# Retention's output projection in three rounded products, with norm and gate written in place

## The chip, the cores and the metric
The kernel runs on one core of a Trainium2 chip. A core has a matrix engine (TensorE, PE in the profile; its weight loads are PEld), a vector engine (VectorE, DVE), a scalar engine (ScalarE, ACT), GpSimd (POOL) and a queue that starts transfers (SyncE, SP). Each runs its own instructions in order and waits for the others through semaphores. The metric is the device time of one execution in microseconds; the median of three runs of the kernel before is 1364.03 us (1363.96 to 1365.25).

## The reference, cut to what matters
The program is a block of four layers on x of shape (4, 1024, 256): retention, a mixture of experts, a recurrence, and a mixture of experts again. Only retention is touched by the change:

```python
x = x + retention(layernorm(x))          # x: (4, 1024, 256)
# retention(x):
qkv = x @ w_qkv.T ; q, k, v = split(qkv) # 16 heads of 16; q, k rotated by position
scores = q k^T * 16**-0.5 * decay mask   # causal, decaying by head
y = scores @ v
yn = (y - mean) / sqrt(var + 1e-5)       # over (16 channels, 1024 tokens) of a head and batch
yn = yn * gn_weight + gn_bias
out = silu(x @ w_gated.T) * yn
return out @ w_proj.T
```

The statistics of the group norm run over all 1024 tokens of a batch element, so norm, gate and output projection of one batch element can't begin before its last token is done.

## The kernel before
Everything is float32 in memory. Tokens are handled in 32 tiles of 128, eight tiles (t = 0 to 7) to each of the four batch elements (b = 0 to 3); i counts tiles over all. Each engine has a hand-written order, a loop over i, in the function `retention`.

TensorE's loop, for tile i: transpose the normed x (L422), outputs of tile i-2 (state products L518, score by value products L524, into the PSUM bank ps_yp), project tile i to q, k (L444, L448) and v (L454), scores of tile i-1 (L484), the gate of tile i (L462), transposes of the rotated q and k (L473). The projections to q, k, v are already done "by parts": x and the weights are each a rounded part (high, type float32r, which TensorE takes in one pass) and a rest (low, the difference, also rounded), and three products are added, high by high, high by low, low by high. High parts of x are made by ScalarE (L345) together with the plain copy (L347); VectorE makes the low part (`x_low`, L623) from both; TensorE needs it at L448.

VectorE's loop: add the state product, norm the next tile's x (L616), rotate q and k (L634, L636; GpSimd adds the two halves, L291, before TensorE may transpose), add a finished pair of the projection to x (L725), mask the scores (L643), statistics, spread q (`spread_q`, L651), `x_low` of the next tile (L623).

While batch b runs, batch b-1 is finished: the group norm's statistics at t = 1 to 3; at t = 4 ScalarE writes the normed values (`normed`, L388, four instructions of 128x512, two before the gate's output and two after the q/k copy L373) into a buffer ynorm, and VectorE multiplies them by the gate (`gated`, L719): the first half after the mask, the second half after x_low of the next tile. At t = 5, 6, 7 and once more at t = 7 TensorE projects a pair of tiles (`projection`, L541), with plain float32 products of ynorm and w_proj; each such product is recorded as two matmuls. y itself lies in yt, double-buffered by batch. The last batch is finished behind the loop, with the PSUM banks of the scores.

Beside this the experts' weights are split for the next layer in 12 pieces: SP loads a piece, ScalarE rounds it at the end of its tile when i is odd, 5 to 27 (`split_high`, L380), GpSimd subtracts at the end of its tile when i is even, 6 to 28 (`split_low`, L305), and SP stores both parts.

Of the kernel before, what the change touches and what calls it, by code (L numbers as in the profile page):

```python
# [11 lines left out]
P = 128  # L12
# [14 lines left out]
def one_pass(ap):  # L27
    return ap.bitcast(mybir.dt.float32r)
# [23 lines left out]
def retention(nc, d, x, x_loaded, x_stats, w_split, home):  # L52
    with ExitStack() as ctx:
# [14 lines left out]

        qk_high, qk_low = (sb(f"qk_{n}", [P, KT, 2 * C]) for n in ("high", "low"))
        v_high, v_low = (sb(f"v_{n}", [P, KT, C]) for n in ("high", "low"))  # L70
        w_gate = sb("w_gate", [P, KT, C])
        w_proj = sb("w_proj", [P, KT, C])
        rope_cos = sb("rope_cos", [P, TPB, 2 * C])
# [28 lines left out]
        state_add = sb("state_add", [P, KT, PAIR])  # L102
        yt = sb("yt", [P, 2, KT, T])
        silu_g = sb("silu_g", [P, 2, KT, T])
        ynorm = sb("ynorm", [P, KT, T])
        gn_stats = sb("gn_stats", [P, KT, 2, 6])
        gn_sum = sb("gn_sum", [P, KT])
        gn_dev = sb("gn_dev", [P, KT, 4])
# [62 lines left out]
        gn_root = sem("gn_root")  # L171
        ynorm_ready = sem("ynorm_ready")
        gated_ready = sem("gated_ready")
        out_in_psum = sem("out_in_psum")
        x_added = sem("x_added")
        x_stats_ready = sem("x_stats_ready")
# [50 lines left out]
        with nc.Block() as block:  # L227
# [43 lines left out]
            @block.gpsimd  # L271
            def _(pool):
                pool.memset(expo[:], -0.5).then_inc(zeroed, 1)
                pool.memset(v_heads[:], 0.0).then_inc(zeroed, 1)
                pool.wait_ge(zeroed, 2)

                def ln_root_first():
                    pool.wait_ge(first_moments, MOMENT_STEPS)
                    pool.tensor_tensor(rstd[:, 0:1], vare[:, 0:1], expo[:, 0:1], ALU.pow).then_inc(first_rstd, 1)

                def ln_root(b):
                    own = slice(1 if b == 0 else 0, TPB)
                    pool.wait_ge(ln_moments, (b + 1) * MOMENT_STEPS)
                    pool.tensor_tensor(rstd[:, own], vare[:, own], expo[:, own], ALU.pow).then_inc(ln_rstd, 1)

                def sum_rotation(i):
                    pool.wait_ge(rope_parts, (i + 1) * 3)
                    if i >= 2:

                        pool.wait_ge(y_in_psum, i - 1)  # L290
                    pool.tensor_tensor(roped[:, i % 2, :], rope_t1[:], rope_t2[:], ALU.add).then_inc(rope_done, 1)  # L291

                def sum_state(i):
                    pool.wait_ge(state_masked, states_before(i + 1))

                    pool.wait_ge(y_in_psum, i + 1)
                    pool.tensor_tensor(state[:], state[:], state_add[:], ALU.add).then_inc(state_ready, 1)

                def gn_inverse_root(b):
                    pool.wait_ge(gn_step, b * GN_STEPS + 9)  # L300
                    pool.tensor_tensor(gn_rstd[:], gn_vare[:], expo[:, 0:KT], ALU.pow).then_inc(gn_root, 1)

                def split_low(n):
                    pool.wait_ge(w_high_ready, n + 1)
                    pool.tensor_tensor(one_pass(w_low[:, n % 2, :]), w_raw[:, n % 2, :], w_high[:, n % 2, :],  # L305
                                       ALU.subtract).then_inc(w_low_ready, 1)

                def split_weights_low():
                    pool.wait_ge(qkv_high_ready, 2)
                    pool.tensor_tensor(one_pass(qk_low[:]), w_qk[:], qk_high[:], ALU.subtract).then_inc(qkv_low_ready, 1)  # L310
                    pool.tensor_tensor(one_pass(v_low[:]), w_v[:], v_high[:], ALU.subtract).then_inc(qkv_low_ready, 1)

                def state_of(i):
                    return i >= 0 and i % TPB not in (0, TPB - 1)

                ln_root_first()
                ln_root(0)
                for i in range(TILES):
                    b, t = step_of(i)
                    if t == TPB - 2 and b < B - 1:  # L320
                        ln_root(b + 1)
                    if state_of(i - 2):
                        sum_state(i - 2)
                    sum_rotation(i)
                    if i == 0:
                        split_weights_low()
                    if t == 3 and b > 0:
                        gn_inverse_root(b - 1)
                    if 6 <= i < 6 + 2 * PIECES and i % 2 == 0:
                        split_low(i // 2 - 3)  # L330
                sum_state(TILES - 2)
                gn_inverse_root(B - 1)

            @block.scalar
            def _(act):
# [14 lines left out]
                def y_out(i):  # L350
                    b, t = step_of(i)
                    act.wait_ge(y_in_psum, i + 1)
                    act.activation(yt[:, b % 2, :, t * P:(t + 1) * P], ps_y.rearrange("p (k t) -> p k t", k=KT),
                                   ACT.Copy).then_inc(yt_ready, 1)

# [26 lines left out]
                def normed(b, n):  # L382

                    act.wait_ge(gn_step, (b + 1) * GN_STEPS)
                    if b > 0:
                        act.wait_ge(out_in_psum, b * PAIRS)
                    for k in range(KT):
                        act.activation(ynorm[:, k, n * HALF:(n + 1) * HALF], yt[:, b % 2, k, n * HALF:(n + 1) * HALF],  # L388
                                       ACT.Identity, bias=gn_shift[:, k:k + 1], scale=gn_scale[:, k:k + 1]) \
                            .then_inc(ynorm_ready, 1)  # L390

                act.preload_act_table_set("silu_and_others")
                act.wait_ge(zeroed, 2)
                for i in range(TILES):
                    b, t = step_of(i)
                    x_transposed(i)
                    if i == 0:
                        split_weights_high()
                    if i >= 2:
                        y_out(i - 2)  # L400
                    v_out(i)
                    if b > 0 and t == 4:
                        normed(b - 1, 0)
                    gate_out(i)
                    qk_out(i)
                    if b > 0 and t == 4:
                        normed(b - 1, 1)
                    if 5 <= i < 5 + 2 * PIECES and i % 2 == 1:
                        split_high((i - 5) // 2)
                y_out(TILES - 2)  # L410
# [5 lines left out]
            def _(pe):  # L416
# [116 lines left out]
                def group_variance(b):  # L533
                    pe.wait_ge(gn_step, b * GN_STEPS + 8)
                    pe.matmul(ps_yp[:, 0:KT], head_mean[:], gn_var[:], start=True, stop=True).then_inc(gn_sums, 1)

                def projection(b, pair, into):
                    pe.wait_ge(gated_ready, b * 4 + (2 if pair < PAIRS // 2 else 4))
                    for n in range(2):
                        for k in range(KT):  # L540
                            mm = pe.matmul(into[:, n * C:(n + 1) * C], ynorm[:, k, (2 * pair + n) * P:(2 * pair + n + 1) * P],  # L541
                                           w_proj[:, k, :], start=(k == 0), stop=(k == KT - 1))
                    mm.then_inc(out_in_psum, 1)

                pe.wait_ge(first_consts_loaded, 16 * len(first_consts))
                for i in range(TILES):
                    b, t = step_of(i)
                    transpose_x(i)
                    if i >= 2:
                        outputs(i - 2)  # L550
                    project(i)
                    if i == TPB - 1:
                        pe.wait_ge(consts_loaded, 16 * len(consts))
                    if b > 0 and t in (2, 3, 5, 6, 7):

                        pe.wait_ge(yt_ready, i - 1)
                    if b > 0 and t == 2:
                        group_mean(b - 1)
                    if b > 0 and t == 3:
                        group_variance(b - 1)  # L560
                    if b > 0 and t >= 5:
                        projection(b - 1, t - 5, ps_yp)
                    if i >= 1:
                        scores(i - 1)
                    gate(i)
                    if b > 0 and t == TPB - 1:
                        pe.wait_ge(x_added, b * PAIRS - 1)
                        projection(b - 1, PAIRS - 1, ps_yp)
                    transpose_qk(i)
                outputs(TILES - 2)  # L570
                scores(TILES - 1)
# [15 lines left out]
            def _(dve):  # L587
# [126 lines left out]
                def gated(b, n):  # L714
                    dve.wait_ge(gate_ready, (b + 1) * TPB)
                    dve.wait_ge(ynorm_ready, b * 4 + 2 * n + 2)
                    for k in range(KT):
                        half = slice(n * HALF, (n + 1) * HALF)
                        dve.tensor_tensor(ynorm[:, k, half], ynorm[:, k, half], silu_g[:, b % 2, k, half], ALU.mult) \  # L719
                            .then_inc(gated_ready, 1)  # L720

                def add_out(b, pair, source):
# [2330 lines left out]
```

## Time and profile before

| | |
|---|---|
| median of 3 runs | 1364.03 us |
| profiled execution | 1364.07 us |
| its span, first to last instruction | 1362.3 us |
| mean granted TensorE clock | 0.935 |
| busy: PE, DVE, ACT, POOL | 84%, 68%, 45%, 41% |
| PE line of the retention's 12 rebuilt pairs (L541, ret_ps_yp) | 96 matmuls of 379 ns |

The profile page cuts the span in 40 slices; the retention stage is the first nine of them, about 305 us. A timeline row reads: start, duration, engine, line, operation, output<-inputs, shape, count of merged instructions, and in brackets the idle time before it with what ended it. Durations of one instruction include the time that it is held after issue. Consecutive instructions on VectorE and ScalarE overlap by some 0.1 us, so an instruction's pitch is a little shorter than its duration.

### The profile page before, as it was taken

To read this page: it belongs to the slowest core of one execution; us is meant where nothing else is said; L and a number is where in the kernel's file an instruction comes from. 1 tells how busy PE (TensorE), PEld (TensorE's weight loads), DVE (VectorE), ACT (ScalarE), POOL (GpSimd) and SP (SyncE) were. 2 spreads that over 40 slices of the span, in tenths; PEclk is the share of its full clock that TensorE was granted. 3 is DMA by queue.
4 is the path that set the end of the run, shared out by engine and by line. 5 is a ranking of instruction groups with operands and counts; after the bars stand their busy time and mean duration, and the time that the engine had idled before them with its cause. 6 is when DMAs were issued, how large, how long until landed. Compare 5 with 4: busy or idle time off the path is not lost. (4 is left out here: it accounts for less than half of the span.)

```text
span 1362.3 us, 35045 instructions
## 1 busy us (share of the span) xinstructions
PE 1148.7 (84%) x14041; PEld 817.2 (60%) x14041; DVE 929.0 (68%) x1959; ACT 612.8 (45%) x1310; POOL 552.3 (41%) x537
## 2 busy tenths in 40 slices
PE   7999999964799998578989889898996647999970
PEld 4667777753688886235555555555554436888860
DVE  6778887757756565657778695968756276655646
ACT  3343343413355554153737355564634233555544
POOL 3333333202477775314161432415141014777750
PEclk9999999987799999687999999999999778999995
DMA  8122222009643332100000001000000095333339
GB/s 306 62 97 95 94 94 79 33 0 370 192 170 103 102 104 82 62 31 3 32 4 32 7 29 34 3 33 3 1 3 3 3 379 185 105 102 105 101 97 350
DMA packets 50684, 125.68 MB, mean 92 GB/s; under 512 B 7648, under 2 KB 26976, under 8 KB 47712
## 3 DMA queue, kind: packets, MB, share of 16 engines
q1 hardware_dynamic: 36896, 86.20, 17.7%
q0 software_dynamic: 13632, 37.24, 8.7%
q8 instruction: 117, 1.92, 0.6%
q14 instruction: 39, 0.32, 0.1%
HBM read 79.63 MB, written 43.78 MB: 91 GB/s over the span
## 5 line engine op out<-in xcount | busy, mean ns | idle before, releaser
L1108 POOL DMA_INDIRECT ffn_xs<-xn_rows,ffn_from_row x142 | 137.6, 969 | 122.2 <-DVE ffn_second_y_at L1490 79.5
L1116 POOL DMA_INDIRECT y_rows<-ffn_ys,ffn_to_row x142 | 140.2, 987 | 55.3 <-issue 35.8
L1271 PE MATMUL ffn_ps_h<-ffn_w_high,ffn_xst 128*128 x568 | 156.2, 397 | 0.7 <-issue 0.7
L1518 DVE TENSOR_TENSOR ffn_act_in<-ffn_silu_g,ffn_ps_h 128x256 f32<-128x256 f32 x142 | 59.8, 421 | 139.9 <-ACT ffn_silu_g L1150 139.9
L1150 ACT ACTIVATE ffn_silu_g<-ffn_ps_h 128x256 f32<-128x256 f32 x142 | 54.5, 384 | 145.4 <-PE ffn_ps_h L1271 145.4
L1291 PE MATMUL ffn_ps_o<-ffn_w,ffn_act_t 128*128 x284 | 116.4, 433 | 0.5 <-DVE ffn_act_t L1523 0.5
L1271 PEld LDWEIGHTS ffn_ps_h<-ffn_w_high,ffn_xst 128*128 128x128 f32 x568 | 97.5, 190 | 18.9 <-issue 1.2
L1870 POOL TENSOR_TENSOR rec_mixed_w<-rec_mixed_w,rec_xnt 128x512 f32<-128x512 f32 x16 | 17.2, 1090 | 212.4 <-DVE rec_mixed_w L2671 212.4
L1271 PE MATMUL ffn_ps_h<-ffn_w_low,ffn_xst 128*128 x284 | 89.5, 397 | 0.0
L643 DVE TENSOR_TENSOR ret_probs<-ret_score,ret_causal 128x2048 f32<-128x2048 f32 x32 | 73.3, 2292 | 18.2 <-PE ret_score L484 18.2
L1293 PE MATMUL ffn_ps_o<-ffn_w,ffn_act_t 128*128 x284 | 79.0, 278 | 0.0
L291 POOL TENSOR_TENSOR ret_roped<-ret_rope_t 128x512 f32<-128x512 f32 x32 | 40.6, 1270 | 78.7 <-DVE ret_rope_t L636 78.7
L2707 DVE TENSOR_TENSOR rec_probs<-rec_core,home 128x1024 f32<-128x1024 f32 x32 | 39.0, 1219 | 43.7 <-PE rec_core L2424 34.5
L1157 ACT ACTIVATE ffn_ys<-ffn_ps_o 128x256 f32<-128x256 f32 x142 | 54.6, 384 | 29.0 <-PE ffn_ps_o L1293 29.0
L1534 DVE TENSOR_TENSOR ffn_ys<-ffn_ys,ffn_ps_o 128x256 f32<-128x256 f32 x142 | 59.8, 421 | 8.3 <-ACT ffn_ys L1157 2.9
L1166 ACT ACTIVATE ffn_xst<-ffn_ps_t 128x256 fp32r<-128x256 f32 x142 | 55.7, 393 | 15.9 <-PE ffn_ps_t L1261 15.9
L1528 DVE TENSOR_TENSOR ffn_xst<-ffn_ps_t,ffn_xst 128x256 fp32r<-128x256 f32 x142 | 59.0, 415 | 3.3 <-ACT ffn_xst L1166 3.3
L1271 PEld LDWEIGHTS ffn_ps_h<-ffn_w_low,ffn_xst 128*128 128x128 f32 x284 | 53.9, 190 | 12.2
L1523 DVE TENSOR_TENSOR ffn_act_t<-ffn_ps_a,ffn_act_t 128x256 fp32r<-128x256 f32 x142 | 59.3, 417 | 0.8 <-ACT ffn_act_t L1162 0.8
L2177 PE MATMUL rec_odd<-rec_mixed_w,home 128*128 128x512 f32 (+1 forms) x96 | 50.2, 655 | 10.4 <-DVE rec_mixed_r L2671 9.0
L1261 PE MATMUL ffn_ps_t<-ffn_constants,ffn_xs 128*128 128x128 f32 x284 | 54.7, 274 | 4.8 <-DMA ffn_xs<-xn_rows,ffn_from_row 3.1
L1291 PEld LDWEIGHTS ffn_ps_o<-ffn_w,ffn_act_t 128*128 128x128 f32 x284 | 53.6, 189 | 7.1 <-issue 1.1
(353 smaller groups left out, 2894.1 us busy)
## 6 DMA issues: line engine op xcount, KB each, us to landing
home<-y_rows SPq DMA_DIRECT2D x30, 512.0 KB, 4.8
w_split<-home SPq DMA_DIRECT2D x24, 512.0 KB, 4.2
ffn_w_high<-w_split SPq DMA_DIRECT2D x8, 1024.0 KB, 9.8
ffn_w_low<-w_split SPq DMA_DIRECT2D x8, 1024.0 KB, 10.3
ffn_w<-w_split SPq DMA_DIRECT2D x8, 1024.0 KB, 14.7
home<-in_f_w SPq DMA_DIRECT2D x12, 512.0 KB, 6.2
xn_rows<-home SPq DMA_DIRECT2D x12, 512.0 KB, 10.8
out<-x SPq DMA_DIRECT2D x8, 512.0 KB, 5.5
```

The source lines that it names most:

```text
L643: dve.tensor_tensor(probs[:].rearrange("p g k h t -> p (g k h) t"), score[:].rearrange("p g (h t) -> p (g h) t", t=P), causal[:].unsqueeze ...
L1108: pool.indirect_dma_start(xs[:, n % SLOTS, :], None, xn_rows[:], bass.IndirectOffsetOnAxis(ap=from_row[:, n:n + 1], axis=0)) \
L1116: pool.indirect_dma_start(y_rows[:], bass.IndirectOffsetOnAxis(ap=to_row[:, m:m + 1], axis=0), ys[:, m % SLOTS, :], None).then_inc(ys_stor ...
L1166: act.activation(one_pass(xst[:, u % 2, 0]), xt_in_bank(u), ACT.Copy).then_inc(xst_high, 1)
L1261: mm = pe.transpose(ps_t[:, u % 2, k * P:(k + 1) * P], xs[:, n % SLOTS, k * P:(k + 1) * P], ident[:])
L1271: mm = pe.matmul(ps_h[:, u % 2, :], one_pass(xst[:, u % 2, part, k, :]), one_pass(w1[w_part][k][:, bass.ds(e, E_COLUMNS)]), start=(part + ...
L1291: pe.matmul(ps_o[:, u % 2, :], one_pass(act_t[:, u % 2, 0, k, :]), one_pass(w), start=(k == 0), stop=False)
L1293: mm = pe.matmul(ps_o[:, u % 2, 0:C], one_pass(act_t[:, u % 2, 1, k, :]), one_pass(w[:, 0:C]), start=False, stop=(k == KT - 1))
L1518: dve.tensor_tensor(act_in[:, u % 2, :], silu_g[:, u % 2, :], ps_h[:, u % 2, FF:2 * FF], ALU.mult) \
L1523: dve.tensor_tensor(one_pass(act_t[:, u % 2, 1]), act_t_in_bank, act_t[:, u % 2, 0], ALU.subtract) \
L1528: dve.tensor_tensor(one_pass(xst[:, u % 2, 1]), xt_in_bank(u), xst[:, u % 2, 0], ALU.subtract) \
L1534: dve.tensor_tensor(ys[:, n % SLOTS, :], ys[:, n % SLOTS, :], ps_o[:, u % 2, C:2 * C], ALU.add).then_inc(ys_ready, 1)
```

## The change
The output projection of batches 0 to 2 is done by parts, like the projections to q, k and v. w_proj is split once: ScalarE rounds it at the end of tile i = 4, GpSimd makes the rest at i = 5. Of the gated values, ScalarE rounds half a batch at the end of its tile t = 4 and the other half at the end of t = 5; GpSimd subtracts after its rotation sum of the same tiles, ahead of the weight piece's subtraction. TensorE's pair then is 12 single-pass matmuls of 256 columns and not 4 plain products (8 recorded matmuls). The buffer ynorm is gone: ScalarE norms yt in place and VectorE gates it in place; the two parts have buffers of their own. The wait for the projection of the batch before moves from the norm to the rounding, and y's first copy of a batch (b >= 2) waits for the last subtraction from that half of yt. The last batch keeps its plain products, now from yt.

```diff
@@ gpsimd
+                def split_projection_low():
+                    pool.wait_ge(proj_high_ready, 1)
+                    pool.tensor_tensor(one_pass(proj_low[:]), w_proj[:], proj_high[:], ALU.subtract).then_inc(proj_low_ready, 1)
+
+                def gated_low(b, n):
+                    half = slice(n * HALF, (n + 1) * HALF)
+                    pool.wait_ge(gated_high_ready, b * 2 + n + 1)
+                    pool.tensor_tensor(one_pass(gated_rest[:, :, half]), yt[:, b % 2, :, half], gated_high[:, :, half], ALU.subtract) \
+                        .then_inc(gated_low_ready, 1)
...
                     sum_rotation(i)
                     if i == 0:
                         split_weights_low()
+                    if i == 5:
+                        split_projection_low()
                     if t == 3 and b > 0:
                         gn_inverse_root(b - 1)
+                    if t in (4, 5) and b > 0:
+                        gated_low(b - 1, t - 4)
                     if 6 <= i < 6 + 2 * PIECES and i % 2 == 0:
                         split_low(i // 2 - 3)
@@ scalar
                     act.wait_ge(y_in_psum, i + 1)
+                    if b >= 2 and t == 0:
+
+                        act.wait_ge(gated_low_ready, (b - 1) * 2)
...
                     act.wait_ge(gn_step, (b + 1) * GN_STEPS)
-                    if b > 0:
-                        act.wait_ge(out_in_psum, b * PAIRS)
                     for k in range(KT):
-                        act.activation(ynorm[:, k, n * HALF:(n + 1) * HALF], yt[:, b % 2, k, n * HALF:(n + 1) * HALF],
+                        act.activation(yt[:, b % 2, k, n * HALF:(n + 1) * HALF], yt[:, b % 2, k, n * HALF:(n + 1) * HALF],
                                        ACT.Identity, bias=gn_shift[:, k:k + 1], scale=gn_scale[:, k:k + 1]) \
                             .then_inc(ynorm_ready, 1)
+
+                def split_projection_high():
+                    act.wait_ge(consts_loaded, 16 * len(consts))
+                    act.activation(one_pass(proj_high[:]), w_proj[:], ACT.Copy).then_inc(proj_high_ready, 1)
+
+                def gated_high_out(b, n):
+                    half = slice(n * HALF, (n + 1) * HALF)
+                    act.wait_ge(gated_ready, b * 4 + 2 * n + 2)
+                    if b > 0:
+
+                        act.wait_ge(out_in_psum, b * PAIRS)
+                    act.activation(one_pass(gated_high[:, :, half]), yt[:, b % 2, :, half], ACT.Copy).then_inc(gated_high_ready, 1)
...
                     if b > 0 and t == 4:
                         normed(b - 1, 1)
+                        gated_high_out(b - 1, 0)
+                    if b > 0 and t == 5:
+                        gated_high_out(b - 1, 1)
+                    if i == 4:
+                        split_projection_high()
                     if 5 <= i < 5 + 2 * PIECES and i % 2 == 1:
                         split_high((i - 5) // 2)
@@ tensor
+                def projection_by_parts(b, pair):
+                    pe.wait_ge(proj_low_ready, 1)
+                    pe.wait_ge(gated_low_ready, b * 2 + (1 if pair < PAIRS // 2 else 2))
+                    for n in range(2):
+                        tokens = slice((2 * pair + n) * P, (2 * pair + n + 1) * P)
+                        for m, (part, w) in enumerate(((gated_high, proj_high), (gated_high, proj_low), (gated_rest, proj_high))):
+                            for k in range(KT):
+                                mm = pe.matmul(ps_yp[:, n * C:(n + 1) * C], one_pass(part[:, k, tokens]), one_pass(w[:, k, :]),
+                                               start=(m + k == 0), stop=(m == 2 and k == KT - 1))
+                    mm.then_inc(out_in_psum, 1)
+
...
                     if b > 0 and t >= 5:
-                        projection(b - 1, t - 5, ps_yp)
+                        projection_by_parts(b - 1, t - 5)
...
                         pe.wait_ge(x_added, b * PAIRS - 1)
-                        projection(b - 1, PAIRS - 1, ps_yp)
+                        projection_by_parts(b - 1, PAIRS - 1)
@@ vector
-                        dve.tensor_tensor(ynorm[:, k, half], ynorm[:, k, half], silu_g[:, b % 2, k, half], ALU.mult) \
+                        dve.tensor_tensor(yt[:, b % 2, k, half], yt[:, b % 2, k, half], silu_g[:, b % 2, k, half], ALU.mult) \
                             .then_inc(gated_ready, 1)
```

## Rows read from the trace of the kernel before

**Rows 1.** Busy time by stretches: us, each engine's busy time, granted clock, DMA share, GB/s.
```profile
138.40:208.10 69.70, 66.74 (x855) 49.81 (x854) 57.33 (x111) 27.73 (x72) 23.99 (x20) 1.00 0.28 92
...
286.00:290.00 4.00, 0.70 (x7) 0.57 (x3) 2.41 (x10) 0.38 (x1) 0.00 (x0) 0.63 0.00 0
```

**Rows 2.** Instructions that read ynorm: duration ns min/median/max, first and last start.
```profile
L541 PE MATMUL ret_ps_yp<-ret_w_proj,ret_ynorm x96: 377/379/382, 113.1 to 277.1; 128*128 128x256 f32 x96
```

**Rows 3.** Timeline, tiles 20 and 21 (t = 4 and 5), 176 to 187 us.
```profile
176.09 2.29 DVE L643 TENSOR_TENSOR ret_probs<-ret_score,ret_causal 128x2048 f32<-128x2048 f32 x1 [0.54 <-PE ret_score L484]
176.88 2.37 POOL L305 TENSOR_TENSOR home<-home 128x1024 fp32r<-128x1024 f32 x1
...
178.30 1.49 DVE L719 TENSOR_TENSOR ret_ynorm<-ret_ynorm,ret_silu_g 128x512 f32<-128x512 f32 x1
...
179.57 0.37 ACT L345 ACTIVATE ret_xnt_high<-ret_ps_xvg 128x256 fp32r<-128x256 f32 x1
...
179.83 0.38 ACT L347 ACTIVATE ret_xnt<-ret_ps_xvg 128x256 f32<-128x256 f32 x1
...
180.32 0.68 DVE L651 TENSOR_TENSOR ret_q_par<-ret_qkt,ret_par_of 128x512 f32<-128x512 f32 x1
...
180.92 0.41 DVE L623 TENSOR_TENSOR ret_xnt_low<-ret_xnt,ret_xnt_high 128x256 fp32r<-128x256 f32 x1
...
181.26 1.28 DVE L719 TENSOR_TENSOR ret_ynorm<-ret_ynorm,ret_silu_g 128x512 f32<-128x512 f32 x2
...
181.58 0.64 PE L448 MATMUL ret_ps_qk<-ret_qk_high,ret_xnt_low 128*128 128x512 f32 x2
...
182.05 0.40 PE L454 MATMUL ret_ps_xvg<-ret_v_high,ret_xnt_low 128*128 128x256 f32 x2
...
182.29 0.40 PE L454 MATMUL ret_ps_xvg<-ret_v_high,ret_xnt_high 128*128 128x256 f32 x2
...
182.77 1.89 PE L541 MATMUL ret_ps_yp<-ret_w_proj,ret_ynorm 128*128 128x256 f32 x8
...
183.57 0.68 DVE L634 TENSOR_TENSOR ret_rope_t<-ret_ps_qk,ret_rope_cos 128x512 f32<-128x512 f32 x1
...
184.99 1.27 POOL L291 TENSOR_TENSOR ret_roped<-ret_rope_t 128x512 f32<-128x512 f32 x1 [1.17 <-DVE ret_rope_t L636]
...
186.55 0.47 PEld L473 LDWEIGHTS ret_ps_qkt<-ret_ident,ret_roped 128*128 128x128 f32 x4
```

**Rows 4.** Timeline, tiles 21 and 22 (t = 5 and 6), 187 to 197 us.
```profile
187.79 1.05 ACT L380 ACTIVATE home<-home 128x1024 fp32r<-128x1024 f32 x1
...
188.74 0.38 ACT L345 ACTIVATE ret_xnt_high<-ret_ps_xvg 128x256 fp32r<-128x256 f32 x1
...
189.49 0.43 DVE L623 TENSOR_TENSOR ret_xnt_low<-ret_xnt,ret_xnt_high 128x256 fp32r<-128x256 f32 x1
...
191.21 0.63 PE L448 MATMUL ret_ps_qk<-ret_qk_high,ret_xnt_low 128*128 128x512 f32 x2
...
191.87 0.69 DVE L634 TENSOR_TENSOR ret_rope_t<-ret_ps_qk,ret_rope_cos 128x512 f32<-128x512 f32 x1
...
193.80 1.27 POOL L291 TENSOR_TENSOR ret_roped<-ret_rope_t 128x512 f32<-128x512 f32 x1
...
196.18 0.47 PEld L473 LDWEIGHTS ret_ps_qkt<-ret_ident,ret_roped 128*128 128x128 f32 x4
```

**Rows 5.** Timeline of GpSimd and VectorE, 13 to 18.2 us: instructions that meet.
```profile
13.96 2.40 POOL L310 TENSOR_TENSOR ret_qk_low<-ret_w_qk,ret_qk_high 128x1024 fp32r<-128x1024 f32 x1
15.45 1.45 DVE L651 TENSOR_TENSOR ret_q_par<-ret_qkt,ret_par_of 128x512 f32<-128x512 f32 x1 [1.30 <-ACT ret_qkt L373]
16.32 1.71 POOL L311 TENSOR_TENSOR ret_v_low<-ret_w_v,ret_v_high 128x512 fp32r<-128x512 f32 x1
16.83 1.35 DVE L616 TENSOR_SCALAR ret_xn<-x,ret_mean,ret_rstd 128x256 f32<-128x256 f32 x1
```

**Rows 6.** Timeline, tile 5 in the first batch: its rotation.
```profile
49.12 0.69 DVE L634 TENSOR_TENSOR ret_rope_t<-ret_ps_qk,ret_rope_cos 128x512 f32<-128x512 f32 x1 [1.76 <-PE ret_ps_qk L448]
```

More of the change, by code:

```diff
@@ L70, in retention @@
         v_high, v_low = (sb(f"v_{n}", [P, KT, C]) for n in ("high", "low"))
+        proj_high, proj_low = (sb(f"proj_{n}", [P, KT, C]) for n in ("high", "low"))
         w_gate = sb("w_gate", [P, KT, C])
@@ L104, in retention @@
         silu_g = sb("silu_g", [P, 2, KT, T])
-        ynorm = sb("ynorm", [P, KT, T])
+        gated_high = sb("gated_high", [P, KT, T])
+        gated_rest = sb("gated_rest", [P, KT, T])
         gn_stats = sb("gn_stats", [P, KT, 2, 6])
@@ L173, in retention @@
         gated_ready = sem("gated_ready")
+        gated_high_ready = sem("gated_high_ready")
+        gated_low_ready = sem("gated_low_ready")
+        proj_high_ready = sem("proj_high_ready")
+        proj_low_ready = sem("proj_low_ready")
         out_in_psum = sem("out_in_psum")
@@ L384, in normed @@
                     act.wait_ge(gn_step, (b + 1) * GN_STEPS)
+                    for k in range(KT):
+                        act.activation(yt[:, b % 2, k, n * HALF:(n + 1) * HALF], yt[:, b % 2, k, n * HALF:(n + 1) * HALF],
+                                       ACT.Identity, bias=gn_shift[:, k:k + 1], scale=gn_scale[:, k:k + 1]) \
+                            .then_inc(ynorm_ready, 1)
+                def split_projection_high():
[4 more added lines that the diff above has]
+                    act.wait_ge(gated_ready, b * 4 + 2 * n + 2)
                     if b > 0:
                         act.wait_ge(out_in_psum, b * PAIRS)
-                    for k in range(KT):
-                        act.activation(ynorm[:, k, n * HALF:(n + 1) * HALF], yt[:, b % 2, k, n * HALF:(n + 1) * HALF],
-                                       ACT.Identity, bias=gn_shift[:, k:k + 1], scale=gn_scale[:, k:k + 1]) \
-                            .then_inc(ynorm_ready, 1)
+                    act.activation(one_pass(gated_high[:, :, half]), yt[:, b % 2, :, half], ACT.Copy).then_inc(gated_high_ready, 1)
                 act.preload_act_table_set("silu_and_others")
@@ L535, in group_variance @@
                     pe.matmul(ps_yp[:, 0:KT], head_mean[:], gn_var[:], start=True, stop=True).then_inc(gn_sums, 1)
+                def projection_by_parts(b, pair):
[4 more added lines that the diff above has]
+                        for m, (part, w) in enumerate(((gated_high, proj_high), (gated_high, proj_low), (gated_rest, proj_high))):
+                            for k in range(KT):
+                                mm = pe.matmul(ps_yp[:, n * C:(n + 1) * C], one_pass(part[:, k, tokens]), one_pass(w[:, k, :]),
+                                               start=(m + k == 0), stop=(m == 2 and k == KT - 1))
+                    mm.then_inc(out_in_psum, 1)
                 def projection(b, pair, into):
@@ L540, in projection @@
                         for k in range(KT):
-                            mm = pe.matmul(into[:, n * C:(n + 1) * C], ynorm[:, k, (2 * pair + n) * P:(2 * pair + n + 1) * P],
+                            mm = pe.matmul(into[:, n * C:(n + 1) * C], yt[:, b % 2, k, (2 * pair + n) * P:(2 * pair + n + 1) * P],
                                            w_proj[:, k, :], start=(k == 0), stop=(k == KT - 1))
```

## The prediction
> **What bounds the kernel now.** I read four views: the busy time by stretches, to see which engine fills the retention stage; the projection's rows, to count what is replaced; the timeline of one batch boundary, to see what each engine does when the new work arrives; and places where VectorE and GpSimd meet. Only the first stage is touched. In its third batch TensorE is busy 66.74 of 69.70 us and VectorE 57.33, at full clock [rows 1]; whatever delays either for longer than a few tenths moves the end of the stage, and everything behind it follows in order. A tile with a projection lasts 9.63 us, from one low-part product to the next (181.58 to 191.21) [rows 3, 4]. A batch (b, tiles t = 0 to 7) is normed, gated and projected during tiles 4 to 7 of the next one; I follow global tiles 20, 21 and 22, which are t = 4, 5, 6 of the third batch and project the second, and apply the result to all three boundaries between batches.
>
> **What it saves.** A pair is now 8 recorded matmuls of 0.379, 96 for 12 pairs [rows 2]. The one at 182.77 takes 1.89 us [rows 3], that is 7 pitches + 0.379: a pitch of 0.216, 8 x 0.216 = 1.73 us. The new form (rounded by rounded, 256 columns) is the v projection's: two take 0.24 (182.05 to 182.29), pitch 0.12 [rows 3]; 12 x 0.12 = 1.44 us. So 0.29 us a pair, 3.5 us for all 12. A price as of the old form (12 x 0.216 = 2.59, a loss of 0.86 a pair) I exclude, the row being the same operation in type and shape. The last batch keeps its products.
>
> **What it adds.** Per boundary, two rounding copies of 128x1024 on ScalarE, one at the end of tile 4 and one at the end of tile 5, and two subtractions of 128x1024 on GpSimd. Copy: 1.05 us, as L380 of that size [rows 4]; bounds 0.95 (its pitch to L345) and 1.52 (four times the 0.38 for 256 columns [rows 3]). Subtraction: 2.37 as L305 [rows 3]; 2.40 at most by L310 [rows 5], 2.26 at least (twice the 1.13 that L311 ran once let in, below). Both stand ahead of old work in their queues: on ScalarE ahead of the next tile's x copies, whose low part TensorE waits for; on GpSimd the first subtraction waits for the copy with the weight piece's subtraction (L305), state sum and rotation sum queued behind it.
>
> **The hold.** q's spreading (L651), 0.68 alone, took 1.45 when issued at 15.45 under a GpSimd subtraction that ended at 16.36: it ended 0.54 after that. The next GpSimd subtraction (L311), issued 16.32, ended 18.03, 1.13 after L651's end at 16.90; and VectorE's next, L616, issued 16.83, ended only at 18.18 [rows 3, 5]. So instructions that read SBUF alone wait for the other engine's whole instruction, and a waiting one gets in before the other engine's next. L719 shows the same: 1.49 instead of 0.68, done 0.54 after L305 [rows 3]. The mask (L643), with one operand in PSUM, ran its usual 2.29 under L305 [rows 3]. Now L305 hides under that mask; the new subtractions don't.
>
> The Trainium skill (SBUF — State Buffer, "SBUF: two separate sides") calls this port pair an exclusive lock held for the full instruction, also for VectorE instructions with two SBUF inputs against GpSimd; the rows agree in every case quoted. Read as shared bandwidth instead, the held instructions would be stretched about 2.1 times (1.45 / 0.68), x_low by 0.45 and the two gating products by 1.4, and the sum would be about +2 us a boundary, near 1370.
>
> **Tile 20 into 21.** Gating's first half starts at 178.30 as before, but L305 is no longer there (it waits behind the new subtraction), so its two instructions take 1.28 and end at 179.58 instead of 180.39. ScalarE is free at 179.57; copy to 180.65. Next tile's x copies start there instead of 179.57, and x is ready 0.64 later, at 181.3. GpSimd's subtraction runs 180.7 to 183.07. So x_low(21), which needs both x copies, is issued at 181.3 and held: done 183.35 instead of 181.33. TensorE's L448 goes from 181.58 to 183.4: +1.8 already. L305, pending since 183.07, gets in next: 183.35 to 185.72. Gating's second half is behind it: first instruction done 186.26, second 0.60 later, 186.86 instead of 182.54. That is +4.3 for VectorE, and all behind it: rotation 183.57 to 187.9, GpSimd's sum 184.99 to 189.3, done 190.57; TensorE, which had arrived at 186.55 in the old order, starts the q/k transposes at 190.65: **+4.0** [rows 3]. Pair 0's saving is swallowed there. The projection doesn't wait for the rest: needed at about 184.5, there since 183.07.
>
> **Tile 21 into 22.** ScalarE reaches the place of L380 at 191.8; the second rounding comes first, then L380, so x's copies start at 193.7 (188.74 before) and x is ready at 194.35. GpSimd's second subtraction starts at 192.85, held a little by L651 (about 192.6 to 193.3), and runs to 195.65. x_low(22) is held again: done 195.9 instead of 189.92, **+6.0**; TensorE's L448 191.21 to 195.95, +4.75. Rotation, 1.95 after x_low, 197.85; rotation's sum starts 1.93 after that (GpSimd's layer-norm root and state sum are between), 199.8, done 201.05. TensorE's own order would bring it there at +4.75 - 0.29, 200.6; it waits to 201.15, **+5.0** against 196.18 [rows 4].
>
> **The rest of the boundary.** Pairs 2 and 3, both in t = 7, save 0.58. In these tiles VectorE waits for TensorE, so the saving counts but the delay isn't made up: there is no idle TensorE time to make it up from (2.96 in 69.70 [rows 1]). Net +4.4 a boundary, three of them: **+13.2 us**. The boundary into the fourth batch has no L380 behind its second copy, but x_low waits for GpSimd there anyway.
>
> **Edits that I price at nothing.** The rounding of the projection's weights, 128x512 on ScalarE at tile 4, about 0.5 (half of L380; at most 0.76), and its rest on GpSimd at tile 5, 1.27 as L291: the first batch has slack, the rotation waits 1.76 us for TensorE [rows 6], and the rest lies under the mask. Uncovered they cost 0.8 and 1.3 once. Norm and gate in y's buffer change addresses, not kinds of operands: 0, either way. The wait dropped from the norm, and now before the rounding, asks for a projection four tiles earlier: 0. y's new wait (t = 0) asks for a subtraction done over two tiles earlier: 0. The weight piece stored by SP comes 6.5 us later (185.72 against 179.25); its slot is next read two tiles, over 19 us, on: 0, or up to a couple of us where a load would then be late.
>
> Span 1362.3, profiled execution 1364.07, median 1364.03, so no correction: 1364.07 + 13.2 = **1377.3 us**.
>
> **Rivals.**
> - *VectorE keeps the port after x_low(21)*, L305 going behind gating: gating ends 184.6, L305 runs to 186.95 and holds the norm of the next tile instead, rotation at 187.1, +3.5 instead of +4.3; +3.6 a boundary, 1374.9. Against it L311 before L616 [rows 5]. I count it within the forecast.
> - *No hold that matters* (x_low and gating run beside GpSimd): x_low(21) is +0.4, GpSimd's queue (183.07 + 2.37 + the state sum) makes the rotation sum +0.8 and the transposes +0.55; at 22 x_low is +1.45, TensorE +0.6, the transposes +0.4, and two pairs give 0.58 back: 0 in all, 1364. Against it L651 and L719.
> - *It is just cheaper*: copies and subtractions hidden, -3.5 us, 1360.6. It needs ScalarE's copy to be off x's path and the subtraction to end before x is ready; ScalarE's order forbids the first and [rows 5] the second.
> - *The clock falls.* The granted clock is 1.00 in the batch, at its level of 2.4 GHz, and fell in the stage's tail, 0.63 over 286 to 290, where TensorE was busy 0.70 of 4 us [rows 1]. The new waits leave it idle for up to 1.8 us before L448(21) and 2.2 (4.0 - 1.8) before the transposes, within some 10 us. If that takes it to 1.2 GHz for 6 of a tile's 9.63 us of TensorE work, it is 6 more a boundary: 1377 + 18 = 1395. Against it: gaps stand singly between busy stretches.
>
> **Chances.** Forecast with the first rival 0.76, no hold 0.08, cheaper 0.06, clock 0.10. The forecast's own spread: 1374.9 below; above, a copy of 1.52 adds 0.47 twice a boundary, 2.8 in all, 1380; L305 or a load late adds some more. The range of 8 in 10 leaves out the two good cases and most of the clock: 1370 to 1387. A measurement of this kernel tells 0.2% (2.7 us) from nothing: faster 0.06, same 0.08, slower 0.86.
>
> **What would show it.** In the changed kernel's timeline: projections of 12 matmuls in about 1.44 + 0.17 us; x_low at t = 5 and 6 at over 1.5 us instead of 0.41, ending 0.3 after a GpSimd subtraction; gating's second half starting with a 3 us instruction at t = 4; a VectorE-to-GpSimd wait before TensorE's transposes at t = 5; batch lengths up by 4 to 5 us, the last batch's tail as before. x_low at 0.41 beside a running subtraction would refute the hold; the boundary unchanged with x_low held would refute that the path goes through VectorE.

## The result, and the profile after

The changed kernel takes 1383.2 us (median of 4, 1379.1 to 1384.4) against 1364.0 before: ratio 1.0131, 95% interval 1.0101 to 1.0162. Its profiled execution took 1379.09 us with a span of 1377.3: 15.0 over the one before. Predicted were 1377.3 us and +13.2; the median is 19.2 over, so 6 us more than predicted.

The retention stage ends where the experts' first instruction starts, 306.5 us before and 319.8 after (views by tile):

```profile
L1092 POOL MEMSET ffn_expo<- x2: 124/124/125, 306.5 to 1088.6; 128x32 f32 x2
```
```profile
L1142 POOL MEMSET ffn_expo<- x2: 124/124/124, 319.8 to 1102.2; 128x32 f32 x2
```
So the stage pays 13.3 us of the 15.0; 1.4 of the rest stand in the last experts' stage (273.7 us before, 275.1 after), whose code the change doesn't touch. The timeline of the same tiles as [rows 3], t = 4 and 5, all of it late by the 4.87 us that the boundary before had cost:

```profile
183.18 1.28 DVE L769 TENSOR_TENSOR ret_yt<-ret_yt,ret_silu_g 128x512 f32<-128x512 f32 x2
...
184.50 1.06 ACT L424 ACTIVATE ret_gated_high<-ret_yt 128x1024 fp32r<-128x1024 f32 x1
...
185.46 0.37 ACT L366 ACTIVATE ret_xnt_high<-ret_ps_xvg 128x256 fp32r<-128x256 f32 x1
...
185.63 2.36 POOL L327 TENSOR_TENSOR ret_gated_rest<-ret_yt,ret_gated_high 128x1024 fp32r<-128x1024 f32 x1 [3.83 <-ACT ret_gated_high L424]
...
186.20 2.07 DVE L673 TENSOR_TENSOR ret_xnt_low<-ret_xnt,ret_xnt_high 128x256 fp32r<-128x256 f32 x1 [1.14 <-ACT ret_xnt L368]
...
187.95 2.57 POOL L312 TENSOR_TENSOR home<-home 128x1024 fp32r<-128x1024 f32 x1
188.20 2.88 DVE L769 TENSOR_TENSOR ret_yt<-ret_yt,ret_silu_g 128x512 f32<-128x512 f32 x1
...
188.33 0.73 PE L487 MATMUL ret_ps_qk<-ret_qk_high,ret_xnt_low 128*128 128x512 f32 x2 [1.20 <-DVE ret_xnt_low L673]
...
192.71 0.68 DVE L684 TENSOR_TENSOR ret_rope_t<-ret_ps_qk,ret_rope_cos 128x512 f32<-128x512 f32 x1
...
194.13 1.27 POOL L298 TENSOR_TENSOR ret_roped<-ret_rope_t 128x512 f32<-128x512 f32 x1 [1.17 <-DVE ret_rope_t L686]
...
195.44 0.42 PEld L512 LDWEIGHTS ret_ps_qkt<-ret_ident,ret_roped 128*128 128x128 f32 x4 [2.28 <-POOL ret_roped L298]
```
The low part of x (L673, L623 before) takes 2.07 us and ends 0.28 after the subtraction L327. The weight piece's L312, waiting since 187.95, goes next, and gating's first instruction (L769) takes 2.88: it ends 0.56 after L312. TensorE then waits 2.28 for the rotation. The next tile, against [rows 4]:

```profile
197.76 2.58 POOL L327 TENSOR_TENSOR ret_gated_rest<-ret_yt,ret_gated_high 128x1024 fp32r<-128x1024 f32 x1 [2.37 <-ACT ret_gated_high L424]
...
198.53 0.37 ACT L366 ACTIVATE ret_xnt_high<-ret_ps_xvg 128x256 fp32r<-128x256 f32 x1
...
199.28 1.34 DVE L673 TENSOR_TENSOR ret_xnt_low<-ret_xnt,ret_xnt_high 128x256 fp32r<-128x256 f32 x1 [1.18 <-ACT ret_xnt L368]
...
200.68 0.73 PE L487 MATMUL ret_ps_qk<-ret_qk_high,ret_xnt_low 128*128 128x512 f32 x2 [0.45 <-DVE ret_xnt_low L673]
```

One thing is new at the first boundary. Busy time by stretches (us, PE, PEld, DVE, ACT, POOL busy, granted clock, DMA share, GB/s):

```profile
120.00:124.00 4.00, 2.45 (x46) 1.66 (x46) 3.64 (x5) 2.32 (x3) 1.63 (x2) 0.87 0.41 131
124.00:128.00 4.00, 4.00 (x43) 2.73 (x36) 3.11 (x13) 1.10 (x4) 1.85 (x1) 0.71 0.00 0
```
The mean granted clock is 0.87 and 0.71 of the 2.4 GHz level, so part of these 8 us ran at the 1.2 GHz level; before, it was 1.00 in both.

The stage's tail differs too. Behind the last tile TensorE's clock falls in every run; 16 us around that fall, in the kernel before and in the changed one:

```profile
284.00:300.00 16.00, 10.49 (x76) 8.91 (x77) 7.59 (x23) 3.32 (x5) 0.70 (x1) 0.68 0.00 0
```
```profile
296.00:312.00 16.00, 10.39 (x71) 8.35 (x72) 6.84 (x20) 3.31 (x5) 0.70 (x1) 0.57 0.00 1
```
The mean clock is 0.68 before and 0.57 after: the changed kernel spends longer there at the lower level.

For the experiments I use one number per tile, the *lag*: the start of GpSimd's rotation sum of that tile less the same in the kernel before.

| lag, us | tile 12 | 13 | 14 | 16 | 20 | 24 | 28 | 31 | stage end |
|---|---|---|---|---|---|---|---|---|---|
| the change | 0.1 | 4.4 | 5.9 | 4.6 | 4.9 | 9.0 | 9.0 | 12.7 | 13.3 |
| e0 the change again | 0.0 | 4.3 | 5.8 | 4.5 | 4.6 | 8.8 | 8.9 | 13.3 | 13.8 |
| e1 rest: one column | 0.0 | 2.2 | 4.3 | 2.6 | 2.7 | 3.9 | 3.9 | 6.9 | 5.9 |
| e2 piece first | 1.4 | 4.3 | 7.2 | 5.5 | 5.8 | 10.1 | 10.2 | 13.2 | 12.8 |
| e3 rounding: one column | 0.0 | 3.6 | 4.7 | 3.7 | 3.7 | 6.7 | 6.7 | 9.3 | 8.7 |
| e4 products only | 0.1 | 0.1 | -0.2 | -1.1 | -0.9 | -2.0 | -1.9 | -2.6 | -3.1 |
| e5 low part from PSUM | 0.4 | 4.3 | 6.3 | 5.9 | 6.0 | 11.4 | 11.5 | 15.6 | 16.1 |
| e6 under the mask | -0.1 | -0.1 | -0.1 | -0.9 | -0.9 | -1.7 | -1.7 | -2.1 | -2.8 |
| e8 = e2, filled | 0.2 | 3.1 | 5.8 | 4.4 | 4.4 | 8.5 | 8.5 | 12.7 | 13.3 |
| e9 = e5, filled | 0.3 | 4.3 | 4.9 | 3.8 | 3.8 | 7.1 | 7.1 | 10.3 | 10.8 |
| e10 = e6 again | 0.1 | 0.1 | 0.1 | -0.7 | -0.7 | -1.6 | -1.6 | -1.9 | -2.6 |
| e11 = e2, filled once | 0.5 | 3.4 | 5.0 | 3.4 | 3.3 | 6.3 | 6.2 | 9.4 | 9.8 |

A boundary costs the lag at 16 less that at 12, 24 less 20, 31 less 28. The third figure is not quite like the first two: pairs 2 and 3 are projected in t = 7, too late to move the rotation sum of tile 31, so what they save (0.58 by the prediction; the three figures of e4 are -1.2, -1.1 and -0.6) shows only in the column "stage end".

### The profile page after: what moved, and what is told of

Its sections match the earlier page's. It is cut to its first block and busy times, and to the rows that moved or that the text cites. A ratio compares the mean times of both kernels' runs of the same rounds, so it can differ in the third digit from the quotient of the medians.

```text
span 1377.3 us, 35155 instructions
## 1 busy us (share of the span) xinstructions
PE 1150.0 (83%) x14089; PEld 819.6 (60%) x14089; DVE 941.1 (68%) x1959; ACT 619.1 (45%) x1317; POOL 568.9 (41%) x544
## 6 DMA issues: line engine op xcount, KB each, us to landing
ffn_w_low<-w_split SPq DMA_DIRECT2D x8, 1024.0 KB, 11.5
```

## The experiments

**e0, the change unaltered.**

> The changed kernel once more, unaltered. Its profiled run had the retention stage end 13.25 us later than before (first instruction of the experts' stage at 319.77 and not 306.52 us), and its span 15.0 longer; the median of all its runs was 19 longer. If the change costs only what the stage shows, the stage ends at 319.8 again and the whole is 13 to 15 us over the kernel before run beside it. If something behind the stage pays too, the whole is 17 to 20 over it, and the stage end is the same 319.8.

1381.5 us, ratio 1.0107 (1.0069 to 1.0144), stage end 320.3, half a microsecond later. That half lies in the third boundary: it costs 4.4 here and 3.7 in the changed kernel's profile, the same program, with a clock of 0.74 and 0.84 over 268 to 276 us here and 1.00 there. The rest of the spread lies elsewhere: the recurrence stage (first instruction to the second experts' stage), which the change doesn't touch, took 533.2 us before, 533.7 in the changed kernel's profile, 538.3 here, and 529.9 to 535.1 in the others. What stands over 13.3 us in the medians (15.2 here, 19.2 above) is of that size and was not traced further.

**e1, GpSimd's subtraction cut to one column.**
```diff
-  pool.tensor_tensor(one_pass(gated_rest[:, :, half]), yt[..., half], gated_high[:, :, half], ALU.subtract)
+  one = slice(n * HALF, n * HALF + 1)
+  pool.tensor_tensor(one_pass(gated_rest[:, :, one]), yt[..., one], gated_high[:, :, one], ALU.subtract)
...
-  (gated_rest, proj_high)
+  (gated_high, proj_high)
```


> GpSimd's subtraction of the gated rest is cut to one column of each half; TensorE reads the rounded part in its place, so the third product is not the reference's. All waits and both ScalarE copies stay. Hold theory: at t = 4 the weight piece's subtraction, queued behind the small one, takes its place, so the low part of x at tile 21 still takes about 2 us, but nothing is pending then and gating's second half takes 1.28; at t = 5 nothing holds and the low part takes 0.43. Rotation of tile 21 +2.1 (+4.4 in the changed kernel), net +1.2 us a boundary, stage end about 310.2. Copies theory (ScalarE's two copies on x's path are the price, the hold only fills a wait that is there anyway): a boundary keeps nearly its +4.4, stage end 318 to 320.

1373.1 us, ratio 1.0052 (1.0032 to 1.0072). Tile 13 at 2.2 (2.1 expected); the second boundary, at clock 1.00, costs 1.2, as expected. First and third cost 2.6 and 3.0, and there the clock fell (0.78 and 0.80 over 112 to 120 us, 0.70 and 0.88 over 256 to 264). Timeline and stretches at tile 13:

```profile
111.19 2.36 POOL L312 TENSOR_TENSOR home<-home 128x1024 fp32r<-128x1024 f32 x1
...
111.61 2.22 DVE L674 TENSOR_TENSOR ret_xnt_low<-ret_xnt,ret_xnt_high 128x256 fp32r<-128x256 f32 x1 [1.14 <-ACT ret_xnt L369]
...
113.76 1.28 DVE L770 TENSOR_TENSOR ret_yt<-ret_yt,ret_silu_g 128x512 f32<-128x512 f32 x2
...
114.65 0.63 PE L494 MATMUL ret_ps_xvg<-ret_v_high,ret_xnt_low 128*128 128x256 f32 x2
```
```profile
112.00:114.00 2.00, 0.67 (x4) 0.22 (x3) 2.00 (x2) 0.00 (x0) 1.55 (x1) 1.00 0.00 0
114.00:116.00 2.00, 2.00 (x9) 1.86 (x10) 2.00 (x6) 0.00 (x0) 0.10 (x1) 0.56 0.81 328
```
The piece's subtraction holds the low part in place of the one removed, and nothing holds gating. TensorE idles, the clock goes to 0.56, and two v products take 0.63, not 0.40. The copies theory (4.4 a boundary) is out.

**e2, the weight piece first.**
```diff
+  if 6 <= i < 6 + 2 * PIECES and i % 2 == 0: split_low(i // 2 - 3)
   if t in (4, 5) and b > 0: gated_low(b - 1, t - 4)
-  if 6 <= i < 6 + 2 * PIECES and i % 2 == 0: split_low(i // 2 - 3)
```


> One swap in GpSimd's order: the weight piece's subtraction ahead of the gated rest's, so that it lies under the mask again. Nothing is left out. Hold theory: gating's first half is held again (1.49), the low part of x at t = 5 still is, but no instruction is pending behind it, so gating's second half takes 1.28 and not 3.48: rotation at tile 21 +2.9 and not +4.4, about +3.0 us a boundary, stage end 315.6. If the order on GpSimd doesn't matter (the long first instruction of gating is a wait that VectorE would have anyway): 319.8.

1377.8 us, ratio 1.0102 (1.0055 to 1.015). Tile 13 is +2.9 and tile 21 +2.9, as expected, with gating at 1.28; this profile reaches tile 12 1.4 late, 1.3 of it from the stage's first two tiles, where the clock was 0.64 over 12 to 16 us and 1.00 before. But the boundaries cost 4.1, 4.3 and 3.0: only the third, the one with the clock at 1.00, is near the 3.0 expected, and its figure leaves out 0.58 of saving; the clean test is e11. In the first:

```profile
113.65 0.70 PE L483 MATMUL ret_ps_qk<-ret_qk_high,ret_xnt_high 128*128 128x512 f32 x2 [1.28 <-ACT ret_xnt_high L366]
...
116.01 1.22 PE L487 MATMUL ret_ps_qk<-ret_qk_high,ret_xnt_low 128*128 128x512 f32 x2 [1.19 <-DVE ret_xnt_low L673]
```
```profile
112.00:114.00 2.00, 0.72 (x18) 0.44 (x7) 0.86 (x3) 1.82 (x4) 0.69 (x1) 1.00 0.90 356
114.00:116.00 2.00, 0.82 (x4) 0.34 (x2) 2.00 (x2) 0.06 (x1) 1.67 (x1) 0.88 0.91 242
116.00:118.00 2.00, 1.99 (x7) 1.80 (x8) 2.00 (x6) 0.00 (x0) 0.00 (x0) 0.50 0.41 156
```
Held gating makes ScalarE's copy later (1.28 us of waiting for it, against 0.47 in the changed kernel at tile 21), so TensorE waits twice, close together.

**e3, ScalarE's copies cut to one column.**
```diff
-  act.activation(one_pass(gated_high[:, :, half]), yt[..., half], ACT.Copy)
+  act.activation(one_pass(gated_high[:, :, one]), yt[..., one], ACT.Copy)
...
-  pool.tensor_tensor(one_pass(gated_rest[:, :, half]), yt[..., half], gated_high[:, :, half], ALU.subtract)
+  pool.tensor_tensor(one_pass(gated_rest[:, :, half]), yt[..., half], silu_g[..., half], ALU.subtract)
```


> ScalarE's two rounding copies are cut to one column of each half; GpSimd subtracts the gate's values in place of the rounded ones, same sizes, and TensorE reads the rest in place of the rounded part, so the projection of three batches is not the reference's. Hold theory: the subtraction only starts some 1 us earlier and still holds: low part of x at t = 5 about 1.9 to 2.1 us, gating's first instruction about 2.9; rotation at tile 21 +3.4; net +2.2 a boundary, stage end about 313.2. Copies theory: with the copies gone the price is gone, only the saving of 0.29 a pair is left, stage end 303 to 304.

1378.1 us, ratio 1.0108 (1.007 to 1.0146). The hold without the copies: 3.7, 3.0, 2.6 a boundary, stage end 315.2; the first had a clock of 0.68 and 0.89 over 120 to 128 us, the other two 1.00. Tile 21 is +3.6 (3.4 expected). The miss, 3.0 for 2.2 at the second boundary, fits another victim (not tested by itself): at t = 5 the subtraction, 1 us earlier, catches q's spreading:

```profile
195.04 2.36 POOL L327 TENSOR_TENSOR ret_gated_rest<-ret_yt,ret_silu_g 128x1024 fp32r<-128x1024 f32 x1 [1.52 <-ACT ret_gated_high L425]
...
195.56 2.39 DVE L702 TENSOR_TENSOR ret_q_par<-ret_qkt,ret_par_of 128x512 f32<-128x512 f32 x1
```

**e4, the products by themselves.**
```diff
-  projection(b - 1, t - 5, ps_yp)
+  projection_by_parts(b - 1, t - 5)   # both calls; products (qk_high, qk_high), (qk_high, qk_low), (qk_low, qk_high)
```


> The kernel before with nothing but the twelve pairs exchanged for 12 single-pass products each, of the rounded q/k weights with themselves (as tiles that are there anyway): no copy, no subtraction, no new wait; the projection of three batches is not the reference's. It measures the term of the saving by itself. If all pairs are on the path: 0.29 x 12 = 3.5 us, stage end 303.0 and not 306.5, the whole 3.5 less. If VectorE or the rotation sum is as late as TensorE in these tiles, half of it or less: stage end 304.8 or later.

Stage end 303.4: 3.1 us for twelve pairs, 0.26 a pair. The whole shows no difference it could tell, 1362.9 us, ratio 0.9996 (0.9969 to 1.0022).

**e5, the low part from PSUM.**
```diff
-  dve.tensor_tensor(one_pass(xnt_low[:, i % 2, :, :]), xnt[:, i % 2, :, :], xnt_high[...], ALU.subtract)
+  dve.tensor_tensor(one_pass(xnt_low[:, i % 2, :, :]), ps_xt.rearrange("p (k t) -> p k t", k=KT), xnt_high[...], ALU.subtract)
```


> The changed kernel with one operand of x's low part taken from the PSUM tile of the transposes and not from its SBUF copy (same values, same waits). By the hold as I read it (only instructions that read SBUF alone are held) it then takes about 0.42 beside GpSimd's subtraction and TensorE doesn't wait for it. But gating's second half then meets the subtraction: it is held by it, and its second instruction by the weight piece's. Rotation at tile 21 +4.0, net +3.4 a boundary, stage end about 316.7. Rival: the held low part is the price: with it gone, +1 a boundary, stage end 309.5. If reading PSUM doesn't free it, it takes 2.07 again and the stage ends at 319.8.

1385.4 us, ratio 1.0153 (1.0113 to 1.0194). Thirty low parts, none held, while gating still is (view by tile: duration ns min/median/max):
```profile
L673 DVE TENSOR_TENSOR ret_xnt_low<-ret_ps_xvg,ret_xnt_high x30: 411/424/427, 23.2 to 285.4; 128x256 fp32r<-128x256 f32 x30
```
```profile
L769 DVE TENSOR_TENSOR ret_yt<-ret_yt,ret_silu_g x16: 680/690/2859, 109.0 to 311.8; 128x512 f32<-128x512 f32 x16
```
Tile 13 is +3.9, as expected, but the boundaries cost 5.5, 5.4 and 4.1, not 3.4, with this clock:
```profile
120.00:124.00 4.00, 2.48 (x44) 1.76 (x46) 3.60 (x5) 2.34 (x3) 1.63 (x2) 0.75 0.52 153
124.00:128.00 4.00, 4.00 (x38) 2.45 (x30) 2.27 (x12) 1.08 (x4) 2.61 (x2) 0.50 0.01 4
```

**e8, e9, e11: keep TensorE busy through the waits.** e8 is e2 with both fillers, e9 is e5 with both, e11 is e2 with the first alone.
```diff
+  if i >= TPB and i % TPB in (5, 6):
+      for _ in range(12 if i % TPB == 5 else 4): pe.transpose(score[:, 0, 0:P], ident[:], ident[:])
   pe.wait_ge(xnt_low_ready, i - WHOLE + 1)
...
-  pe.wait_ge(rope_done, i + 1)   # first of the three waits
...
+  if i >= TPB and i % TPB == 5:
+      for _ in range(14): pe.transpose(ps_qkt[:, 0:P], ident[:], ident[:])
+  pe.wait_ge(rope_done, i + 1)
```


> The granted clock was seen to fall behind the new waits: with the weight piece first, to 0.63 over 116 to 120 us and 0.83, 0.75 over 188 to 196, while the third boundary kept 1.00; these boundaries cost 4.1, 4.5 and 3.1 us. Here that kernel gets dummy transposes of the identity where TensorE waits at t = 5 and 6 (12 and 4 ahead of the low part, 14 ahead of the q/k transposes at t = 5), into PSUM that is free. If the idle time takes the clock down and the fall costs the rest: 1.00 throughout, each boundary 3.0 to 3.3 us. Rival: the two dearer boundaries are dear by their transfers or by another wait, and the clock only follows: they stay at 4 us or more. A filler that comes out longer than the wait would cost some tenths in all three.

> The same fillers in the kernel that takes the low part from PSUM; there the clock was at 0.75, 0.50 and 0.89 over 120 to 132 us, 0.64 and 0.51 over 196 to 204, 0.57 over 272 to 276, and the boundaries cost 5.5, 5.5 and 4.2. If the clock is what was missing in my expectation of 3.4 a boundary: 1.00 throughout, 3.2 to 3.8 us each, stage end 317 to 318 and not 322.6. Rival: the low part from PSUM costs TensorE or ScalarE something by itself, and the boundaries stay above 4.5.

> The weight piece first, with the fillers ahead of the low part only. In the run with both, the 14 ahead of the q/k transposes ended 1.5 us after the rotation sum was there (119.65 and 121.16 us) and so stood on the path. Without them, and with the clock kept at 1.00: about 3.0 us a boundary, stage end 315.5 to 316.5. Rival: with the piece first a boundary costs 4 us by itself, whatever the clock: 319.

In all three the clock is 1.00 at every boundary. e9: 3.5, 3.3, 3.2 a boundary, stage end 317.3, 5.3 us earlier than e5 with dummy work added; ratio 1.0063 (1.0043 to 1.0084), where e5 had 1.0153. e8 (1377.2 us, ratio 1.0097, 1.0062 to 1.0131) missed its number: 4.2, 4.1, 4.2. With the clock kept up TensorE came to the second filler at 119.63, when the rotation sum was done at 119.65, so there was next to nothing left to wait for and the 1.69 us stood on the path:
```profile
118.37 1.28 POOL L298 TENSOR_TENSOR ret_roped<-ret_rope_t 128x512 f32<-128x512 f32 x1 [1.16 <-DVE ret_rope_t L692]
...
119.63 1.69 PE L515 MATMUL ret_ps_qkt<-ret_ident 128*128 128x128 f32 x14
```
e11 without it: 2.8, 2.9 and 3.1, stage end 316.3, as expected. It ran on another chip, whose experts' stages are longer (before beside it 1453.8 us, this kernel 1467.1), so only its stage and its ratio, 1.0084 (1.0053 to 1.0116), are read.

**e6 and e10, the same arithmetic for pairs 1 to 3 of a batch, under the mask; pair 0 keeps the plain products.** The edit in short:
```diff
-  if t in (4, 5) and b > 0: gated_low(b - 1, t - 4)
+  if t in (5, 7) and b > 0: gated_low(b - 1, (t - 5) // 2)     # pairs 1 and 2; pair 3
...
-  (t == 4) gated_high_out(b - 1, 0)   (t == 5, end of tile) gated_high_out(b - 1, 1)
+  (t == 5, between v_out and gate_out) gated_high_out(b - 1)    # pairs 1 to 3 in one copy
...
+  if t == 5: projection(b - 1, 0, ps_yp)                        # pair 0 plain
+  else: projection_by_parts(b - 1, t - 5)
```


> The change rearranged, nothing left out: pair 0 keeps its plain products; ScalarE rounds the other three pairs' values in one copy at t = 5 between v's and the gate's output, where it idled 3.2 us; GpSimd subtracts pairs 1 and 2 (128x1024) behind the rotation sum of t = 5, under the mask, and pair 3 (128x512) behind that of t = 7. Hold theory: no VectorE instruction is held longer than before, three pairs a boundary save 0.29 each: 2.6 us, stage end 303.9, the whole about 1361.4 beside 1364. Copies theory or any other: the work on ScalarE or GpSimd still costs 1 us or more a boundary, stage end 307 or later.

> The rearranged kernel again, unaltered: its ratio was 0.996 with an interval that reaches 0.9991. The stage ends at 303.7 again; the whole is 2.5 to 6 us below the kernel before beside it, the part over 2.8 being what the recurrence stage happens to take (529.9 us there, 533.2 before, in the same code).

```profile
182.64 1.50 ACT L425 ACTIVATE ret_gated_high<-ret_yt 128x1536 fp32r<-128x1536 f32 x1
...
184.95 2.29 DVE L696 TENSOR_TENSOR ret_probs<-ret_score,ret_causal 128x2048 f32<-128x2048 f32 x1 [0.36 <-PE ret_score L523]
185.30 2.37 POOL L328 TENSOR_TENSOR ret_gated_rest<-ret_yt,ret_gated_high 128x1024 fp32r<-128x1024 f32 x1
...
187.81 0.68 DVE L704 TENSOR_TENSOR ret_q_par<-ret_qkt,ret_par_of 128x512 f32<-128x512 f32 x1
...
188.56 0.43 DVE L676 TENSOR_TENSOR ret_xnt_low<-ret_xnt,ret_xnt_high 128x256 fp32r<-128x256 f32 x1
```
The copy lies in ScalarE's idle time, the subtraction under the mask, which runs its usual 2.29, and nothing behind is held. Stage end 303.7 and 303.9; 1360.0 us, ratio 0.996 (0.9929 to 0.9991), and again 1362.5, ratio 0.9981 (0.9961 to 1.0). The stage is 2.6 to 2.8 us shorter in both; in the whole, the second interval reaches no change.

One more view bounds the hold. The prediction's words, that instructions which read SBUF alone wait, are too wide. In the kernel before, the group norm's statistics (L677) read yt in SBUF alone and run beside the weight piece's subtraction:

```profile
60.30 2.37 POOL L305 TENSOR_TENSOR home<-home 128x1024 fp32r<-128x1024 f32 x1
61.23 1.27 DVE L677 BATCH_NORM_STATS2 ret_gn_stats<-ret_yt 128x6 f32<-128x512 f32 x2
```
```profile
L677 DVE BATCH_NORM_STATS2 ret_gn_stats<-ret_yt x16: 675/680/694, 61.2 to 287.2; 128x6 f32<-128x512 f32 x16
```
None of the sixteen is held. Held were the instructions with two tensors in SBUF (low part of x, gating, q's spreading) and, in [rows 5], the norm L616, which has one, and a mean and a root for each partition. Why it is held and the statistics aren't, no run shows.

## Why the prediction was right

- *Saving.* Priced at 0.29 a pair, measured 0.26 (e4).
- *Where the delay starts.* Rotation of tile 21 +4.3 predicted; lag 9.14 less 4.87 is 4.27. Transposes +4.0; 195.44 less 186.55 less 4.87 is 4.02. The hold of these instructions and the order in which the port was passed on (subtraction, low part, piece, gating) came as read from [rows 5]; e1, e2 and e5 each took one link out, and tile 13 moved as expected from the hold (2.2, 2.9 and 3.9). "Instructions that read SBUF alone" was too wide, without weight in the sum: the statistics aren't held.
- *Second subtraction.* Low part of tile 22 +6.0 predicted, 5.8 measured; L448's place +4.75, measured 4.6; transposes +5.0, measured 4.8. The low part itself took 1.34 us, not the "over 1.5" named as a sign.
- *Sum.* 4.4 a boundary, 13.2 in all, against 13.3; the agreement is closer than the terms. Measured are 4.5, 4.1 and 3.7, 0.3 of drift up to tile 12 and between the boundaries, and 0.5 in the tail, where the third boundary's pairs should have given back 0.6. So the price of a boundary at full clock was put some 0.3 too high (second), and the third is over 1 us cheaper than predicted, but the clock, which the sum had at nothing, adds about 0.4 at the first and about 1.1 in the tail. That 1.1 is an estimate: from tile 31 to the stage's end the lag falls by 0.4 to 1.0 in the six runs whose tail has the clock of before (e1 to e4, e6, e10) and grows by 0.4 to 0.6 in the changed kernel, e0, e5, e8, e9 and e11, where it is lower; no run changes the tail by itself. That these errors cancel is luck.
- *The third boundary.* I had taken it for a copy of the second. Its rotation sum at t = 5 is as late (+4.3), but no next batch's statistics (L593, 0.74 us) stand before the rotation there, so in the kernel before TensorE began its transposes 1.06 us after the rotation sum's end and not 0.40: of the delay only 3.3 reaches them, not the second boundary's 3.9. The missing layer-norm root at t = 6, ahead of the rotation sum, fits the rest, about 0.3. Neither was tested by itself.
- *Rivals.* "No hold" and "cheaper" are refuted for this placement. That VectorE keeps the port is refuted (L312 before L769). "The clock falls" I priced at 18 us and set against the forecast, as if one excluded the other; it happens beside the hold, behind its waits, and it is small: in the changed kernel's profile at the first boundary, where it costs about the 0.4 by which that is dearer than the second, and in the tail; in e0 at the third boundary too (0.7). It costs 1.3 and 1.4 at two boundaries of e2 (e11 beside it; the third, at 1.00 in both, differs by 0.1) and 5.3 over the stage in e5 (with e9).
- *Edits at nothing.* Tile 12 has lag 0.1: splitting the weights is hidden.
- *Left over.* The median is 4 us over the profiled run, inside the range; e0 puts a difference of that size in the recurrence stage, without a cause. What the median has over the stage's 13.3 stays unexplained.

The Trainium skill (SBUF — State Buffer, "SBUF: two separate sides") has this lock, for instructions with two SBUF inputs. e5 agrees: one input moved to PSUM, and the longest low part went from 2275 ns to 427.

## What to carry to other kernels

Before giving an elementwise pass to GpSimd because it is idle, list what VectorE runs in the same microseconds: what reads two SBUF tensors, and the norm (one), stood still here for the whole pass (the batch-norm statistics did not), and a second pass queued on GpSimd gets in before VectorE's next instruction. Put such passes under a long VectorE instruction with a PSUM operand (here the mask): in the retention stage that turned 13.3 us lost into 2.6 to 2.8 gained, with nine of the twelve pairs by parts. Price a new TensorE wait with the clock it may lose (0.4 us at the changed kernel's first boundary, up to 2.1 in e5 against e9), and look at the clock of each stretch before calling an experiment a miss.

## What the hardware showed that I had not expected

The hold has no preference for small work: an instruction of 0.43 us (the low part of x) took 2.27. TensorE's clock fell behind pairs of waits of 1.2 to 1.3 us a few microseconds apart (e2, busy 0.72 and 0.82 of 2 us) and stayed at 1.00 in e11, where 1.47 us of transposes filled the second of them. At the third boundary it fell in e0 and not in the changed kernel's profile, the same program, so only boundaries at equal clock can be compared. Dummy work that kept TensorE busy ended the stage 5.3 us earlier (e9 against e5).
